# All matrix products with plain float32 operands in a low-pass convolution block

## The chip, the cores and the metric

The kernel runs on one core of a Trainium2 chip. The metric is the time of one execution on the device in microseconds (us). Before the change the median of three runs is 2578.18 us (2577.39 to 2587.52).

## The reference, cut to what matters

```python
xs = jnp.einsum('bhwc,dc->bhwd', x, W1) + b1      # x (16, 64, 64, 768) f32, W1 (192, 768)
xs = jax.nn.gelu(xs, approximate=False)
xs = fft_low(xs)    # |inverse 2-D FFT of the masked, shifted 2-D FFT| over h and w, per image and channel
xs = jnp.einsum('bhwd,cd->bhwc', xs, W2) + b2     # W2 (768, 192)
return x + xs
```

All tensors are float32. The mask keeps the 32 x 32 lowest frequencies, so the low-pass filter is a 64 x 64 matrix along w, another along h, and a rank-few correction (called corner in the code).

## The kernel before, in words

An image has 4096 positions of 768 channels. It is worked in 16 *pairs* of 128-position tiles (`PAIRS`), so there are 256 pairs over 16 images. A product with TensorE (PE) takes a stationary operand of up to 128 x 128 (loaded by a weight load, row PEld) and a moving operand of so many columns.

*Stage 1* (per pair, in three *units* of four 128-channel chunks, `UPP` = 3, `BLOCKS` = 4). `transpose_unit` (L254) transposes four 128 x 128 pieces of x with PE (L267) into one PSUM bank. ScalarE (ACT) copies the bank to `xt_hi` in the type fp32r (L373, `xt_hi_unit`), VectorE (DVE) computes the rest `xt_lo` (L461). `mm1_unit` (L270) then takes, for every chunk, one product of `xt_hi` with 384 columns (W1 high and W1 low side by side, L280) and one of `xt_lo` with 192 columns (W1 high, L281). Six chunks make one tile of the 192 hidden channels; there are twelve chunks in a pair. DVE adds the halves and b1 (L470, L475), ACT applies Gelu twice (L379, L380) to get `hid_hi` and the full value, DVE makes `hid_lo` (L480).

*Filter along w* (`filter_w_pair`, L284): three products of 384 columns (L290 to L292). ACT copies the result out (L385), SyncE (SP) writes it to DRAM (L201), and when all 16 pairs of an image are there it is read back with h and w swapped (`read_cols`, L208) in eight chunks. *Filter along h* (`filter_h_pair`, L304): three products of 128 columns with operands in **plain float32** (L314 twice, L316 once), the only ones beside the small corner sums (L298, L300) that are plain before the change. DVE adds the correction (L495).

*Stage 2*: ACT takes absolute values into `oa_hi`, `ob`, `ob1`, `y_abs` (L393 to L398), DVE makes the low parts (L502, L504, `split_lo_pair`), and `out_half` (L318) takes five products of 384 columns for each of the four output halves of a pair (L326, L327, L328, L331, L334). The bias b2 is a row of `w2b_lo`. DVE adds x (L513), SP stores (L221).

*Order.* Each engine runs a list written out by hand (`turn`): for step s of a turn and j = 0, 1, 2. `stage(i, s, lag)` gives the image and the pair that a stage works on at this step: stage 1 has lag 0, Gelu and filter w lag 1, reading back lag 17, filter h lag 18, low parts lag 19, output lag 20, store lag 21. In a full step PE runs in this order: at j = 0 a transpose unit (two units ahead), a first-product unit, one output half, filter h; at j = 1 a transpose unit, a first-product unit, filter w, one output half; at j = 2 a transpose unit, a first-product unit, two output halves. So PE works on two images at once. `turns` writes out the turns of images 0, 1 and 15 and the drain (turns 16 and 17); images 2 to 14 run in a hardware loop of 13 rounds. In turn 16 PE has only filter h and output. SP is one queue for all transfers: in a step it loads x for stage 1, stores, reads x for the addition (`load_xc`), issues the next read-back chunk at every second step, and writes filtered rows; a wait of any of them holds the ones behind.

Setup: W1, W2, b2 and the filter land in slots of `xc`, ACT and DVE split them into high and low parts there (L362, L364, L429 to L453), and the first loads of `xc` wait for that (`s_setup`).

Of the kernel before, what the change touches and what calls it, by code (L numbers as in the profile page):

```python
# [10 lines left out]
P = 128  # L11
# [21 lines left out]
SPLIT_LO = FILTER_H + 1  # L33
OUT = FILTER_H + 2
# [4 lines left out]
def lowpass_kernel(nc, x, w1t, b1, w2t, b2, identity, filter_w, filter_h, corner_table, out):  # L39
# [9 lines left out]
    with ctx:  # L49
# [10 lines left out]
        w1s = sb("w1s", [P, KC, 2 * D], F32R)  # L60
        w2a_hi = sb("w2a_hi", [P, C], F32R)
        w2a_lo = sb("w2a_lo", [P, C], F32R)
        w2b_hi = sb("w2b_hi", [P, C], F32R)
        w2b_lo = sb("w2b_lo", [P, C], F32R)
        ident = sb("ident", [P, P])
        b1_rows = sb("b1_rows", [P, D])
        fw_hi = sb("fw_hi", [P, P], F32R)
        fw_lo = sb("fw_lo", [P, P], F32R)
        fh = sb("fh", [P, P])
        corner_pat = sb("corner_pat", [P, 16])  # L70
        xt_hi = sb("xt_hi", [P, XT_SLOTS, BLOCKS * P], F32R)
        xt_lo = sb("xt_lo", [P, XT_SLOTS, BLOCKS * P], F32R)
        hid = sb("hid", [P, 2, 2, D])
        hid_hi = sb("hid_hi", [P, 2, 2, D], F32R)
        hid_lo = sb("hid_lo", [P, 2, 2, D], F32R)
# [5 lines left out]
        y_abs = sb("y_abs", [P, 2, 3, P])  # L81
        oa_hi = sb("oa_hi", [P, O_SLOTS, 2, P], F32R)
        oa_lo = sb("oa_lo", [P, O_SLOTS, 2, P], F32R)
        ob = sb("ob", [P, O_SLOTS, 2, P], F32R)
        ob1 = sb("ob1", [P, O_SLOTS, 2, P], F32R)


        w1f = xc[:, 7, :, :].rearrange("p t (k d) -> p (t k) d", d=D)[:, 0:KC, :]
        w2af, w2bf, b2f, fwf = xc[:, 0, 0, :], xc[:, 0, 1, :], xc[:, 1, 0, :], xc[:, 1, 1, 0:P]
# [13 lines left out]
        s_w1s = sem("w1_ready")  # L103
        s_w2_hi = sem("w2_hi_ready")
        s_setup = sem("setup_done")
        s_chain = sem("setup_chain")
# [7 lines left out]
        s_xhi = sem("xt_hi_ready")  # L114
        s_xlo = sem("xt_lo_ready")
        s_m1 = sem("mm1_unit_done")
        s_sum = sem("hid_summed")
        s_pre = sem("hid_pre_ready")
        s_gelu = sem("gelu_done")
        s_hlo = sem("hid_lo_ready")  # L120
# [9 lines left out]
        s_hi = sem("y_abs_and_hi_ready")  # L130
        s_alo = sem("oa_lo_ready")
        s_blo = sem("ob_lo_ready")
# [36 lines left out]
        def _(sp):  # L169
# [3 lines left out]
            def load_constants():  # L173
                const(fwf, filter_w)
                const(fh[:], filter_h)
                const(corner_pat[:], corner_table)
                const(w2af, w2t[0:P, :])
                for r in range(2):
                    const(w2bf[r * DB:(r + 1) * DB], w2t[P:D, :])
                for r in (64, 96):  # L180
                    const(b2f[r:r + 1], b2.rearrange("(a c) -> a c", a=1))
# [69 lines left out]
        def _(pe):  # L251
            pe.wait_ge(s_ident, 16)

            def transpose_unit(m, n):  # L254
# [8 lines left out]
                until(pe, s_xlo, UNITS, m, n - 1)  # L263
# [6 lines left out]
            def mm1_unit(m, n):  # L270
                if whole(m) and m == 0 and n == 0:
                    pe.wait_ge(s_w1s, 1)
                until(pe, s_xlo, UNITS, m, n + 1)
                for b in range(BLOCKS):
                    t, k = divmod(BLOCKS * n + b, KC)
                    if k == 0:
                        until(pe, s_pre, 2 * PAIRS, m, t - 1)
                    hi = xt_hi[:, n % XT_SLOTS, b * P:(b + 1) * P]
                    lo = xt_lo[:, n % XT_SLOTS, b * P:(b + 1) * P]
                    nc.tensor.matmul(ps_h[t % 2][:, 0:2 * D], hi, w1s[:, k, :], start=k == 0, stop=False)  # L280
                    ins = nc.tensor.matmul(ps_h[t % 2][:, D:2 * D], lo, w1s[:, k, 0:D], start=False, stop=k == KC - 1)  # L281
                ins.then_inc(s_m1, 1)

            def filter_w_pair(m, q):  # L284
                if whole(m) and m == 0 and q == 0:
                    pe.wait_ge(s_setup, 1)
                until(pe, s_hlo, PAIRS, m, q + 1)
                until(pe, s_fs, PAIRS, m, q)
                hi, lo = (t[:, q % 2, :, :].rearrange("p t d -> p (t d)") for t in (hid_hi, hid_lo))
# [28 lines left out]
            def out_half(m, r, u):  # L318
# [4 lines left out]
                a_hi, a_lo, b, b1h = (t[:, r % O_SLOTS, v, :] for t in (oa_hi, oa_lo, ob, ob1))  # L323
# [5 lines left out]
                if u == 0:  # L329
                    until(pe, s_alo, PAIRS, m, r + 1)  # L330
                nc.tensor.matmul(o, a_lo, w2a_hi[:, n], start=False, stop=False)  # L331
                if u == 0:
                    until(pe, s_blo, PAIRS, m, r + 1)
                nc.tensor.matmul(o, b, w2b_hi[:, n], start=False, stop=True).then_inc(s_o, 1)  # L334
# [23 lines left out]
        def _(act):  # L358
            def set_up_hi(q):
                act.wait_ge(s_const, 16 * 8)  # L360
                if q == 1:
                    nc.scalar.activation(w2a_hi[:], w2af, ACT.Copy).then_inc(s_w2_hi, 1)  # L362
                else:
                    nc.scalar.activation(w2b_hi[:], w2bf, ACT.Copy).then_inc(s_w2_hi, 1)  # L364

            def xt_hi_unit(m, n):
# [6 lines left out]
                nc.scalar.activation(xt_hi[:, n % XT_SLOTS, :], ps_xt[n % 2][:], ACT.Copy).then_inc(s_xhi, 1)  # L373

            def gelu_pair(m, q):
                until(act, s_pre, 2 * PAIRS, m, 2 * q + 2)
                until(act, s_f, PAIRS, m, q - 1)
                pre = hid[:, q % 2, :, :]
                nc.scalar.activation(hid_hi[:, q % 2, :, :], pre, ACT.Gelu)  # L379
# [7 lines left out]
            def split_hi_pair(m, r):  # L387
# [3 lines left out]
                until(act, s_blo, PAIRS, m, r - 1)  # L391
                yr, hi, hi1 = y[:, r % 2, :, :], ob[:, r % O_SLOTS, :, :], ob1[:, r % O_SLOTS, :, :]
                nc.scalar.activation(oa_hi[:, r % O_SLOTS, :, :], yr[:, 0:2, :], ACT.Abs)  # L393
                nc.scalar.activation(hi[0:DB, 0, :], yr[0:DB, 2, :], ACT.Abs)
                nc.scalar.activation(hi[DB:P, 1, :], yr[DB:P, 2, :], ACT.Abs)
                nc.scalar.activation(hi1[0:DB, 0, :], yr[0:DB, 2, :], ACT.Abs)
                nc.scalar.activation(hi1[0:DB, 1, :], yr[DB:P, 2, :], ACT.Abs)
                nc.scalar.activation(y_abs[:, r % 2, :, :], yr, ACT.Abs).then_inc(s_hi, 1)  # L398

            def turn(i, count):  # L400
                for s in range(count):
                    for j in range(UPP):
                        if whole(i) and i == 0 and s == 0 and j == 0:
                            for n in range(AHEAD):
                                xt_hi_unit(0, n)
                        if at := stage(i, s, 0):
                            xt_hi_unit(at[0], UPP * at[1] + j + AHEAD)
# [4 lines left out]
                        if j == 2 and (at := stage(i, s, FILTER_H)):  # L412
                            split_hi_pair(*at)
                        if whole(i) and i == 0 and s in (1, 2) and j == 2:
                            set_up_hi(s)
# [4 lines left out]
        def _(dve):  # L420
            chain = [0]

            def link(ins):
                chain[0] += 1
                ins.then_inc(s_chain, 1)
                dve.wait_ge(s_chain, chain[0])

            dve.wait_ge(s_w1, 16)
            link(nc.vector.tensor_copy(w1s[:, :, 0:D], w1f))  # L429
            nc.vector.tensor_tensor(w1s[:, :, D:2 * D], w1f, w1s[:, :, 0:D].bitcast(F32), ALU.subtract).then_inc(s_w1s, 1)  # L430

            def set_up_filters():
                dve.wait_ge(s_const, 16 * 8)
                link(nc.vector.tensor_copy(fw_hi[:], fwf))
                nc.vector.tensor_tensor(fw_lo[:], fwf, fw_hi[:].bitcast(F32), ALU.subtract).then_inc(s_setup, 1)

            def set_up_w2():
                nc.vector.memset(ob1[DB:P, :, :, :].bitcast(F32), 1.0)
                link(nc.vector.memset(w2b_lo[DB:P, :].bitcast(F32), 0.0))

            def set_up_w2a_lo():
                dve.wait_ge(s_w2_hi, 2)
                nc.vector.tensor_tensor(w2a_lo[:], w2af, w2a_hi[:].bitcast(F32), ALU.subtract)

            def set_up_w2b_lo():
                nc.vector.tensor_tensor(w2b_lo[0:DB, :], w2bf[0:DB], w2b_hi[0:DB, :].bitcast(F32), ALU.subtract)

            def set_up_b2_hi():
# [188 lines left out]
```

## Time and profile before

| | |
|---|---|
| runs | 2577.39, 2578.18, 2587.52 us |
| profiled execution, its own time | 2587.09 us |
| its span in the trace | 2585.3 us |
| mean granted TensorE clock | 0.985 |
| busy share of the span | PE 96%, PEld 95%, DVE 77%, ACT 49%, POOL (GpSimd) 14% |
| DMA | 710.34 MB, mean 275 GB/s |

The span is the time from the first to the last recorded instruction. A row of a group says line, engine, operation, output<-inputs, shapes, count, then busy us in all and mean ns of one, then idle time of the engine before them. PE products are pipelined: the duration of one is longer than the distance between the starts of two, and their ends are modelled, so what a product costs in a stream is read from starts, or from the chain, where a piece lasts until the next begins. A plain float32 product in the code stands in the trace as two records (L316: 256 products, 512 records); an fp32r product as one (L280: 3072 products, 3072 records).

### The profile page before, as it was taken

To read this page: it belongs to the slowest core of one execution; us is meant where nothing else is said; L and a number is where in the kernel's file an instruction comes from. 1 tells how busy PE (TensorE), PEld (TensorE's weight loads), DVE (VectorE), ACT (ScalarE), POOL (GpSimd) and SP (SyncE) were. 2 spreads that over 40 slices of the span, in tenths; PEclk is the share of its full clock that TensorE was granted. 3 is DMA by queue.
4 is the path that set the end of the run, shared out by engine and by line. 5 is a ranking of instruction groups with operands and counts; after the bars stand their busy time and mean duration, and the time that the engine had idled before them with its cause. 6 is when DMAs were issued, how large, how long until landed. Compare 5 with 4: busy or idle time off the path is not lost.

```text
span 2585.3 us, 55397 instructions
## 1 busy us (share of the span) xinstructions
PE 2479.2 (96%) x16736; PEld 2444.6 (95%) x16736; DVE 2000.3 (77%) x4123; ACT 1271.2 (49%) x3076; POOL 349.4 (14%) x628
## 2 busy tenths in 40 slices
PE   8999999999999999999999999999999999999977
PEld 7899999999999999999999999999999999999976
DVE  6688887878878787787878878788787887888855
ACT  4555554555545455454544545455454554555532
POOL 1211111111111111111111111111111111111100
PEclk9999999999999999999999999999999999999988
DMA  6688887888878788787887878778787887888775
GB/s 198 221 281 289 286 292 258 299 279 283 298 259 292 258 294 286 260 282 270 291 287 258 298 255 291 268 275 294 264 287 266 290 294 258 296 292 285 254 271 228
DMA packets 233562, 710.34 MB, mean 275 GB/s; under 512 B 18706, under 2 KB 85522, under 8 KB 233236
## 3 DMA queue, kind: packets, MB, share of 16 engines
q1 hardware_dynamic: 233236, 706.40, 77.9%
q8 instruction: 154, 2.52, 0.4%
q14 instruction: 172, 1.41, 0.2%
HBM read 454.67 MB, written 251.66 MB: 273 GB/s over the span
## 4 chain that ended last, share of the span: by engine, by line
PE 88%; DMA 4%; issue 4%; ACT 1%; DVE 1%; SPq 0%; POOL 0%; DVEq 0%; ACTq 0%; POOLq 0%
PE ps L280 21%; PE ps L267 12%; PE ps L281 10%; PE ps L326 7%; PE ps L328 7%; PE ps L327 6%; PE ps L331 6%; PE ps L334 6%; PE ps L314 4%; DMA cols<-filtered_rows 4%; PE ps L290 2%; PE ps L316 2%; PE ps L291 2%; PE ps L292 2%; DVE hid_lo L480 0%
## 5 line engine op out<-in xcount | busy, mean ns | idle before, releaser
L373 ACT ACTIVATE xt_hi<-ps 128x512 fp32r<-128x512 f32 x768 | 459.2, 598 | 1205.2 <-PE ps L267 1170.9
L280 PE MATMUL ps<-w1s,xt_hi 128*128 128x384 f32 x3072 | 987.6, 377 | 0.0
L461 DVE TENSOR_TENSOR xt_lo<-ps,xt_hi 128x512 fp32r<-128x512 f32 x768 | 529.9, 690 | 360.1 <-ACT xt_hi L373 346.7
L281 PE MATMUL ps<-w1s,xt_lo 128*128 128x192 f32 x3072 | 773.6, 252 | 0.0
L513 DVE TENSOR_TENSOR xc<-ps,xc 128x384 f32<-128x384 f32 x1024 | 569.4, 556 | 140.9 <-PE ps L334 118.7
L281 PEld LDWEIGHTS ps<-w1s,xt_lo 128*128 128x128 f32 x3072 | 591.1, 192 | 0.0
L280 PEld LDWEIGHTS ps<-w1s,xt_hi 128*128 128x128 f32 x3072 | 582.6, 190 | 0.0
L267 PE MATMUL ps<-ident,xa 128*128 128x128 f32 x3072 | 467.1, 275 | 25.0 <-issue 16.4
L267 PEld LDWEIGHTS ps<-ident,xa 128*128 128x128 f32 x3072 | 378.6, 142 | 46.1 <-issue 26.3
L326 PE MATMUL ps<-w2a_hi,oa_hi 128*128 128x384 f32 x1024 | 365.5, 357 | 0.4 <-DVE xc L513 0.4
L328 PE MATMUL ps<-w2b_lo,ob 128*128 128x384 f32 x1024 | 352.0, 344 | 0.0
L331 PE MATMUL ps<-w2a_hi,oa_lo 128*128 128x384 f32 x1024 | 351.1, 343 | 0.0
L327 PE MATMUL ps<-w2a_lo,oa_hi 128*128 128x384 f32 x1024 | 350.9, 343 | 0.0
L334 PE MATMUL ps<-w2b_hi,ob 128*128 128x384 f32 x1024 | 349.6, 341 | 0.0
L555 POOL TENSOR_TENSOR diff<-hid 128x192 f32<-128x192 f32 x240 | 151.4, 631 | 1103.4 <-ACT hid L380 1103.2
L504 DVE TENSOR_TENSOR ob<-y_abs,ob 64x128 fp32r<-64x128 f32 x512 | 252.8, 494 | 11.4
L559 POOL TENSOR_TENSOR corner_acc<-corner_acc,diff 128x192 f32<-128x192 f32 x240 | 142.9, 595 | 736.7 <-DMA cols<-filtered_rows 726.1
L326 PEld LDWEIGHTS ps<-w2a_hi,oa_hi 128*128 128x128 f32 x1024 | 195.7, 191 | 4.0 <-DVE xc L513 0.8
L327 PEld LDWEIGHTS ps<-w2a_lo,oa_hi 128*128 128x128 f32 x1024 | 197.0, 192 | 0.0
L475 DVE TENSOR_TENSOR hid<-ps,hid 128x192 f32<-128x192 f32 x512 | 183.1, 358 | 17.6
L334 PEld LDWEIGHTS ps<-w2b_hi,ob 128*128 128x128 f32 x1024 | 195.6, 191 | 0.0
L328 PEld LDWEIGHTS ps<-w2b_lo,ob 128*128 128x128 f32 x1024 | 195.4, 191 | 0.0
(50 smaller groups left out, 2714.5 us busy)
## 6 DMA issues: line engine op xcount, KB each, us to landing
xa<-x_dram SPq DMA_DIRECT2D x256, 768.0 KB, 4.8
xc<-x_dram SPq DMA_DIRECT2D x256, 768.0 KB, 7.0
out_dram<-xc SPq DMA_DIRECT2D x256, 768.0 KB, 5.1
filtered_rows<-filt SPq DMA_DIRECT2D x256, 192.0 KB, 2.1
cols<-filtered_rows SPq DMA_DIRECT2D x128, 384.0 KB, 7.4
xc<-w1t_dram SPq DMA_DIRECT2D x1, 576.0 KB, 6.0
xc<-w2t_dram SPq DMA_DIRECT2D x1, 384.0 KB
xc<-w2t_dram SPq DMA_DIRECT2D x2, 192.0 KB
```

The source lines that it names most:

```text
L267: ins = nc.tensor.transpose(ps_xt[n % 2][:, b * P:(b + 1) * P], src, ident[:])
L280: nc.tensor.matmul(ps_h[t % 2][:, 0:2 * D], hi, w1s[:, k, :], start=k == 0, stop=False)
L281: ins = nc.tensor.matmul(ps_h[t % 2][:, D:2 * D], lo, w1s[:, k, 0:D], start=False, stop=k == KC - 1)
L326: nc.tensor.matmul(o, a_hi, w2a_hi[:, n], start=True, stop=False)
L327: nc.tensor.matmul(o, a_hi, w2a_lo[:, n], start=False, stop=False)
L328: nc.tensor.matmul(o, b1h, w2b_lo[:, n], start=False, stop=False)
L331: nc.tensor.matmul(o, a_lo, w2a_hi[:, n], start=False, stop=False)
L334: nc.tensor.matmul(o, b, w2b_hi[:, n], start=False, stop=True).then_inc(s_o, 1)
L373: nc.scalar.activation(xt_hi[:, n % XT_SLOTS, :], ps_xt[n % 2][:], ACT.Copy).then_inc(s_xhi, 1)
L461: nc.vector.tensor_tensor(xt_lo[:, n % XT_SLOTS, :], ps_xt[n % 2][:], xt_hi[:, n % XT_SLOTS, :].bitcast(F32), ALU.subtract).then_inc(s_xlo, 1)
L504: ins = nc.vector.tensor_tensor(o[other, v, :], yr[own, 2, :], o[own, v, :].bitcast(F32), ALU.subtract)
L513: nc.vector.tensor_tensor(x_half, ps_o[u % 2][:, 0:HALF], x_half, ALU.add).then_inc(s_add, 1)
```

## The change

Every high and low part is gone. The operands are plain float32 tensors, the transposes stay. First product: per chunk one product of 192 columns instead of one of 384 and one of 192. Filter w: one product instead of three. Output half: two products of 384 columns instead of five; the second has 65 rows, row 64 being the bias b2 against a row of ones that DVE writes once. ACT runs one Gelu instead of two and three Abs instead of six; DVE runs one addition for the hidden value instead of two, and none of L461, L480, L502, L504. The output runs one step earlier (lag 19, store lag 20). The constants are loaded straight into their places, nothing is split in setup, and the first `xc` loads wait for nothing. Two waits are added: PE waits once for the ones (`s_ones`) and once for the constants; `hid_pre` now also waits for the filter product two pairs back (`s_f`).

```diff
-SPLIT_LO = FILTER_H + 1
-OUT = FILTER_H + 2
+OUT = FILTER_H + 1
 STORE = OUT + 1
...
-        w1s = sb("w1s", [P, KC, 2 * D], F32R)
-        w2a_hi = sb("w2a_hi", [P, C], F32R)
...
+        w1 = sb("w1", [P, KC, D])
+        w2a = sb("w2a", [P, C])
+        w2b = sb("w2b", [P, C])
...
             def load_constants():
-                const(fwf, filter_w)
+                const(fw[:], filter_w)
...
+                const(w2a[:], w2t[0:P, :])
+                const(w2b[0:DB], w2t[P:D, :])
+                const(w2b[DB:DB + 1], b2.rearrange("(a c) -> a c", a=1))
...
-                if whole(m) and m == 0 and r < XC_SLOTS:
-                    sp.wait_ge(s_setup, 2)
...
             def mm1_unit(m, n):
                 if whole(m) and m == 0 and n == 0:
-                    pe.wait_ge(s_w1s, 1)
-                until(pe, s_xlo, UNITS, m, n + 1)
+                    pe.wait_ge(s_w1, 16)
+                until(pe, s_xt, UNITS, m, n + 1)
...
-                    nc.tensor.matmul(ps_h[t % 2][:, 0:2 * D], hi, w1s[:, k, :], start=k == 0, stop=False)
-                    ins = nc.tensor.matmul(ps_h[t % 2][:, D:2 * D], lo, w1s[:, k, 0:D], start=False, stop=k == KC - 1)
+                    ins = nc.tensor.matmul(ps_h[t % 2][:, 0:D], xt[:, n % XT_SLOTS, b * P:(b + 1) * P], w1[:, k, :],
+                                           start=k == 0, stop=k == KC - 1)
...
-                nc.tensor.matmul(ps_f[:, 0:2 * D], fw_hi[:], hi, start=True, stop=False)
-                nc.tensor.matmul(ps_f[:, 0:2 * D], fw_lo[:], hi, start=False, stop=False)
-                nc.tensor.matmul(ps_f[:, 0:2 * D], fw_hi[:], lo, start=False, stop=True).then_inc(s_f, 1)
+                nc.tensor.matmul(ps_f[:, 0:2 * D], fw[:], hid[:, q % 2, :, :].rearrange("p t d -> p (t d)"),
+                                 start=True, stop=True).then_inc(s_f, 1)
...
                 if u == 0:
-                    until(pe, s_hi, PAIRS, m, r + 1)
-                nc.tensor.matmul(o, a_hi, w2a_hi[:, n], start=True, stop=False)
-                nc.tensor.matmul(o, a_hi, w2a_lo[:, n], start=False, stop=False)
-                nc.tensor.matmul(o, b1h, w2b_lo[:, n], start=False, stop=False)
...
-                nc.tensor.matmul(o, a_lo, w2a_hi[:, n], start=False, stop=False)
...
-                nc.tensor.matmul(o, b, w2b_hi[:, n], start=False, stop=True).then_inc(s_o, 1)
+                    until(pe, s_abs, PAIRS, m, r + 1)
+                nc.tensor.matmul(o, oa[:, r % O_SLOTS, v, :], w2a[:, n], start=True, stop=False)
+                nc.tensor.matmul(o, ob[0:DB + 1, r % O_SLOTS, v, :], w2b[0:DB + 1, n], start=False, stop=True).then_inc(s_o, 1)
...
-            def split_hi_pair(m, r):
+            def abs_pair(m, r):
...
+                nc.scalar.activation(oa[:, r % O_SLOTS, :, :], yr[:, 0:2, :], ACT.Abs)
+                nc.scalar.activation(ob[0:DB, r % O_SLOTS, 0, :], yr[0:DB, 2, :], ACT.Abs)
+                nc.scalar.activation(ob[0:DB, r % O_SLOTS, 1, :], yr[DB:P, 2, :], ACT.Abs).then_inc(s_abs, 1)
...
+            nc.vector.memset(ob[DB:DB + 1, :, :, :], 1.0).then_inc(s_ones, 1)
+
+            def hid_pre(m, t):
                 until(dve, s_m1, UNITS, m, -(-KC * (t + 1) // BLOCKS))
...
                     until(dve, s_acc, PAIRS, m, t // 2 - 1)
+                    until(dve, s_f, PAIRS, m, t // 2 - 1)
+                nc.vector.tensor_tensor(hid[:, t // 2 % 2, t % 2, :], ps_h[t % 2][:, 0:D], b1_rows[:], ALU.add).then_inc(s_pre, 1)
```

## Rows read from the trace of the kernel before

**Rows 1.** The page: span, and busy time, share, instructions of each engine.

```profile
span 2585.3 us, 55397 instructions
...
PE 2479.2 (96%) x16736; PEld 2444.6 (95%) x16736; DVE 2000.3 (77%) x4123; ACT 1271.2 (49%) x3076; POOL 349.4 (14%) x628
```

**Rows 2.** The page: the chain that ended last, share of the span by engine.

```profile
PE 88%; DMA 4%; issue 4%; ACT 1%; DVE 1%; SPq 0%; POOL 0%; DVEq 0%; ACTq 0%; POOLq 0%
```

**Rows 3.** Groups by line and shape on PE: busy us, mean ns | idle before.

```profile
L280 PE MATMUL ps<-w1s,xt_hi 128*128 128x384 f32 x3072 | 987.6, 377 | 0.0
L281 PE MATMUL ps<-w1s,xt_lo 128*128 128x192 f32 x3072 | 773.6, 252 | 0.0
L267 PE MATMUL ps<-ident,xa 128*128 128x128 f32 x3072 | 467.1, 275 | 25.0 <-issue 16.4 <-DMA xa<-x_dram 6.0 <-DVE xt_lo L461 2.5
...
L334 PE MATMUL ps<-w2b_hi,ob 128*128 128x384 f32 x1024 | 349.6, 341 | 0.0
L314 PE MATMUL ps<-fh,cols 128*128 128x128 f32 x1024 | 158.4, 277 | 32.4 <-DMA cols<-filtered_rows 25.9 <-issue 4.6 <-POOL cols_b L569 1.8
L316 PE MATMUL ps<-fh,cols_b 128*128 128x128 f32 x512 | 100.8, 279 | 0.0
```

**Rows 4.** The chain in order of time, one pair in mid-kernel: start us, us, what.

```profile
1000.87 0.43 PE ps L267 x4
1001.30 0.18 PE ps L280
1001.49 0.09 PE ps L281
...
1002.43 0.20 PE ps L326
1002.63 0.18 PE ps L327
...
1003.33 0.44 PE ps L314 x4
1003.77 0.22 PE ps L316 x2
...
1010.34 0.44 PE ps L267 x4
```

**Rows 5.** Timeline, a plain float32 product of 16 columns: start, us, engine, shapes.

```profile
109.75 0.30 PEld L298 LDWEIGHTS ps<-corner_pat,corner_acc 128*128 128x128 f32 x2
109.84 0.31 PE L298 MATMUL ps<-corner_pat,corner_acc 128*128 128x16 f32 x2
```

**Rows 6.** Two stretches: length, busy us (count) by engine, granted clock, DMA share, GB/s.

```profile
1000.00:1010.00 10.00, 10.00 (x70) 9.93 (x69) 8.19 (x17) 5.46 (x15) 0.61 (x1) 1.00 0.89 309
1039.60:1042.80 3.20, 3.20 (x11) 3.11 (x12) 2.26 (x6) 0.00 (x0) 0.00 (x0) 0.50 0.00 0
```

**Rows 7.** The chain in order of time, inside the second of these stretches.

```profile
1040.88 0.32 PE ps L326
```

**Rows 8.** Timeline where the loop goes round: [idle before <- what ended it].

```profile
1028.92 0.52 ACT L398 ACTIVATE y_abs<-y 128x384 f32<-128x384 f32 x1
...
1028.93 0.34 PE L334 MATMUL ps<-w2b_hi,ob 128*128 128x384 f32 x1
...
1030.63 0.65 PE L267 MATMUL ps<-ident,xa 128*128 128x128 f32 x4 [1.36 <-issue]
...
1035.86 0.60 ACT L373 ACTIVATE xt_hi<-ps 128x512 fp32r<-128x512 f32 x1 [6.42 <-PE ps L281]
...
1039.56 0.68 PE L290 MATMUL ps<-hid_hi,fw_hi 128*128 128x384 f32 x1 [4.03 <-DVE hid_lo L480]
```

**Rows 9.** Timeline in the drain: a read-back issued, and the product that needs it.

```profile
2488.17 0.91 SPq L214 DMA_DIRECT2D cols<-filtered_rows  x1
...
2495.75 1.11 PE L314 MATMUL ps<-fh,cols 128*128 128x128 f32 x4 [3.97 <-DMA cols<-filtered_rows]
```

**Rows 10.** The page, DMA queues: packets, MB, share of 16 engines.

```profile
q1 hardware_dynamic: 233236, 706.40, 77.9%
```

**Rows 11.** Timeline at the start: the first product of stage 1.

```profile
11.24 0.67 PE L280 MATMUL ps<-w1s,xt_hi 128*128 128x384 f32 x1
```

More of the change, by code:

```diff
@@ L80, in lowpass_kernel @@
         y = sb("y", [P, 2, 3, P])
[L81 to L89, printed above, removed]
+        oa = sb("oa", [P, O_SLOTS, 2, P])
+        ob = sb("ob", [P, O_SLOTS, 2, P])
         ps = [ctx.enter_context(nc.psum_tensor(f"ps{n}", [P, 512], F32)) for n in range(8)]
@@ L358, in _, with xt_unit @@
         def _(act):
[L359 to L366, printed above, removed]
+            def xt_unit(m, n):
                 if n >= UNITS:
@@ L372, in xt_hi_unit @@
                 until(act, s_m1, UNITS, m, n - XT_SLOTS + 1)
-                nc.scalar.activation(xt_hi[:, n % XT_SLOTS, :], ps_xt[n % 2][:], ACT.Copy).then_inc(s_xhi, 1)
+                nc.scalar.activation(xt[:, n % XT_SLOTS, :], ps_xt[n % 2][:], ACT.Copy).then_inc(s_xt, 1)
             def gelu_pair(m, q):
                 until(act, s_pre, 2 * PAIRS, m, 2 * q + 2)
-                until(act, s_f, PAIRS, m, q - 1)
                 pre = hid[:, q % 2, :, :]
-                nc.scalar.activation(hid_hi[:, q % 2, :, :], pre, ACT.Gelu)
                 nc.scalar.activation(pre, pre, ACT.Gelu).then_inc(s_gelu, 1)
@@ L385, in stage_filtered @@
                 nc.scalar.activation(filt[:, q % 2, :, :].rearrange("p t d -> p (t d)"), ps_f[:, 0:2 * D], ACT.Copy).then_inc(s_fs, 1)
-            def split_hi_pair(m, r):
+            def abs_pair(m, r):
                 until(act, s_o, 4 * PAIRS, m, 4 * (r - O_SLOTS + 1))
                 until(act, s_y, PAIRS, m, r + 1)
[L391 to L398, printed above, removed]
+                yr = y[:, r % 2, :, :]
+                nc.scalar.activation(oa[:, r % O_SLOTS, :, :], yr[:, 0:2, :], ACT.Abs)
+                nc.scalar.activation(ob[0:DB, r % O_SLOTS, 0, :], yr[0:DB, 2, :], ACT.Abs)
+                nc.scalar.activation(ob[0:DB, r % O_SLOTS, 1, :], yr[DB:P, 2, :], ACT.Abs).then_inc(s_abs, 1)
             def turn(i, count):
@@ L412, in turn @@
                         if j == 2 and (at := stage(i, s, FILTER_H)):
-                            split_hi_pair(*at)
-                        if whole(i) and i == 0 and s in (1, 2) and j == 2:
-                            set_up_hi(s)
+                            abs_pair(*at)
             turns(act, turn)
@@ L420, in _ @@
         def _(dve):
[L421 to L448, printed above, removed]
-                nc.vector.tensor_copy(w2b_lo[DB:DB + 1, :], b2f[DB:DB + 1])
-            def set_up_b2_lo():
-                link(nc.vector.tensor_copy(w2b_lo[96:97, :], b2f[96:97]))
-                nc.vector.tensor_tensor(w2b_lo[96:97, :], b2f[96:97], w2b_lo[96:97, :].bitcast(F32), ALU.subtract).then_inc(s_setup, 1)
-            def xt_lo_unit(m, n):
-                if n >= UNITS:
-                    m, n = m + 1, n - UNITS
-                    if whole(m) and m >= IMAGES:
-                        return
-                until(dve, s_xhi, UNITS, m, n + 1)
-                nc.vector.tensor_tensor(xt_lo[:, n % XT_SLOTS, :], ps_xt[n % 2][:], xt_hi[:, n % XT_SLOTS, :].bitcast(F32),
-                                        ALU.subtract).then_inc(s_xlo, 1)
-            def hid_sum(m, t):
+            nc.vector.memset(ob[DB:DB + 1, :, :, :], 1.0).then_inc(s_ones, 1)
+            def hid_pre(m, t):
                 until(dve, s_m1, UNITS, m, -(-KC * (t + 1) // BLOCKS))
@@ L497, in y_pair @@
                                         ALU.add if r % 2 == 0 else ALU.subtract).then_inc(s_y, 1)
-            def split_lo_pair(m, r):
-                until(dve, s_hi, PAIRS, m, r + 1)
-                yr, hi, o = y_abs[:, r % 2, :, :], oa_hi[:, r % O_SLOTS, :, :], ob[:, r % O_SLOTS, :, :]
-                nc.vector.tensor_tensor(oa_lo[:, r % O_SLOTS, :, :], yr[:, 0:2, :], hi.bitcast(F32), ALU.subtract).then_inc(s_alo, 1)
-                for v, (own, other) in enumerate(((slice(0, DB), slice(DB, P)), (slice(DB, P), slice(0, DB)))):
-                    ins = nc.vector.tensor_tensor(o[other, v, :], yr[own, 2, :], o[own, v, :].bitcast(F32), ALU.subtract)
-                ins.then_inc(s_blo, 1)
             def add_half(m, r, u):
```

78 lines of the change are left out of this document (14 added, 64 removed).

## Prediction

> **What bounds the kernel now.** I read the page first. PE is busy for 96% of the span and the next engine, DVE, for 77% [rows 1]; busy PE time alone proves little, since the records of pipelined products overlap, so the chain of waits came second: 88% of it lies on PE, the rest is waiting for DMA and for issue, and DVE and ACT have 1% each [rows 2]. Then the groups on PE by shape [rows 3], and for what a product costs in a stream the chain in order of time over one pair [rows 4]. There PE never waits: a pair lasts from 1000.87 to 1010.34, which is 9.47 us, at full granted clock [rows 6]. 256 pairs x 9.47 = 2424 us. The profiled execution took 2587.1 us, so 163 us lie outside the steady work (start, loop ends, drain). The kernel is bound by PE's stream of columns, and the whole question is what a plain float32 product costs there.
>
> **The pair before, in pieces** [rows 4]. A transpose unit takes 0.43, the four chunks behind it run from 1001.30 to 1002.43, 1.13 us; a unit is 1.56 us and a pair has three, 4.68. An output half runs from 1002.43 to 1003.33, 0.90 us for five products, four halves 3.60. Filter h is 0.44 + 0.22 = 0.66. The rest, 9.47 - 4.68 - 3.60 - 0.66 = 0.53, is filter w with three products. So an fp32r product of 384 columns costs 0.176 to 0.18 us in a stream.
>
> **What a plain product costs.** The trace has them at 128 columns only. Each appears as two records, L314 at 0.44/4 and L316 at 0.22/2, that is 0.11 us a record or pass [rows 4]. Two readings give 0.11. One: the weight load sets it. With 16 columns the two loads lie 0.30 minus one load of 0.19, 0.11 us, apart, though the two passes start only 0.05 apart (0.31 minus 0.26 for one) [rows 5]; so a load costs 0.11 whatever the columns. Two: a pass gives every column two column times; 2 x 128 at 2.4 GHz is 0.107. What tells them apart is how long one record lasts. In fp32r 192 columns last 252 ns and 384 last 341 ns, 0.46 ns a column, so 128 would last 222 ns. The plain pass of 128 columns lasts 277 to 279 ns [rows 3], what fp32r would show at about 250 columns. (The transposes, also on float32, show 275.) That is a modelled end, but it speaks clearly for two column times a pass, four for the product.
>
> The Trainium skill, page "FP8 and Floating Point Precision", section "TensorE Precision Notes", says that true FP32 takes four passes through the array; by it alone a product of 192 columns would be 4 x 192 / 2.4 = 320 ns and one of 384 columns 640 ns, an estimate close to mine below, where fp32r takes a quarter of it. The trace shows two records a product, not four, and 128 columns cannot decide, because the load hides the rate there.
>
> Bounds of a pass. Below: the load, 0.11 us, or one column time at the fp32r price, 0.176 for 384 columns. Above: twice the fp32r price for the same columns, 0.352 for 384 and 0.177 for 192. The fp32r price carries a surcharge: 384 columns at 2.4 GHz are 0.160, and 0.176 is 10% more, while at the granted clock 0.50 (1.2 GHz) the same product takes 0.32, exactly its columns [rows 6, 7]. The plain pass at 128 columns shows at most 0.11 for 0.107, so hardly any surcharge. I take column time plus 0.005 us: 0.165 for 192 columns, 0.325 for 384. Each is longer than a load, so the loads stay hidden beneath.
>
> **The pair after.** Removed: all fp32r products. Stage 1: 12 chunks x 2 passes x 0.165 = 3.96, before 3 x 1.13 = 3.39: +0.57. Output: 4 halves x 2 products x 2 passes x 0.325 = 5.20, before 3.60: +1.60. The second product has 65 rows instead of 128; I give it no discount, since every pass of the trace is priced by columns. Filter w: 2 x 0.325 = 0.65, before 0.53: +0.12. Transposes 3 x 0.44 = 1.31 and filter h 0.66 stay. Sum 3.96 + 5.20 + 0.65 + 1.31 + 0.66 = 11.78 us a pair, x 256 = 3016 us.
>
> **The other engines.** ACT loses one Gelu and three Abs of its 1271 us, DVE five groups of its 2000 us (the low parts and one addition); both had room at 9.47 us a pair (5.0 and 7.8 us) [rows 1] and have more at 11.78. This saving is hidden and worth nothing in steady state. The transfers keep their bytes, 77.9% of 2585 us [rows 10], about 2014 us, over a longer time. The added wait of `hid_pre` for the filter product two pairs back stands for a product that PE finished a step before; behind it on DVE are `y_pair` and the additions, and it costs nothing unless DVE runs a step ahead, which its waits for `s_m1` exclude. The single waits for the ones and constants are over long before their first use. Output one step earlier: PE does the same amount per pair in the same place of the step, its input from ACT (three Abs, ready in j = 2) has two output halves and a unit of cover. The end comes one step earlier, but that step held no more than one pair's work in either case: counted at nothing, with 2 us either way. `xc` loads at the start no longer wait for setup: off PE's path.
>
> **What lies around the steady work** (163 us before).
> - *Loop ends.* Twelve times the loop goes round. There PE sits for 1.4 us, ACT comes back 6.4 us after its last Abs, and filter w then waits 4.0 us for ACT and the DVE backlog, after which PE ran for 3.2 us at half clock and lost 1.6 [rows 6, 8]. About 6.6 us each, 79 in all. After the change ACT ends its step about 2 us before PE (its work in j = 2 is 2.1 us after the transposes, PE's 3.9), so its return falls 2 us earlier, there are no low parts to catch up on, and PE has 0.44 + 1.32 + 1.30 + 0.66 + 0.44 + 1.32 = 5.5 us of work before filter w instead of 4.9. I expect only PE's own 1.5 us to stay: 18 us. If that cover fails, up to 79 again.
> - *Drain.* Read-backs are issued one step ahead. One issued at 2488.17 serves a product at 2495.75, 7.6 us later, and PE stood 4.0 us [rows 9]. An image has eight such reads; seven waits like this one are 28 us, with some clock lost behind each I take 37. A step of PE there grows from 4.3 to 5.9 us and the order of the queue is the same, so a wait of about 1.7 us is left per read, 8 x 1.7 = 14 us.
> - *Start*: the first product comes at 11.24 [rows 11]; it no longer waits for the split of W1, some 3 us less. With the filling of the stages and the first read-back 15 us, before 21. End 5 us. What I could not place is about 20 us; I keep it.
> Sum 18 + 14 + 15 + 5 + 20 = 72. The profiled execution comes to 3016 + 72 = 3088 us. The median of the runs before was 0.35% under the profiled one (2578.18 against 2587.09); that gives 3077, rounded to **3080 us**, 19% slower.
>
> **Rivals.**
> *A, one column time a pass.* If a plain pass streams at one column per cycle, and 0.11 at 128 columns is only the load, a unit is 0.44 + 8 x 0.11 = 1.32, a half 4 x 0.176 = 0.70, filter w 0.35, and the pair 3.96 + 2.82 + 0.35 + 0.66 = 7.8 us, 1995 us in all. Then read-backs come late in every second step (9 us of path against 7.8 of work, some 130 us), the loop ends cost their old 79 and the rest 30: 2230 us, faster. It decides from a pass of 384 columns below about 0.25 us. For it: 0.11 fits the load exactly. Against: 277 ns. Chance 0.07.
> The Trainium skill, page "TensorE: Matmul & The Clock Gate", section "Weight-path perf modes — Fast Weight Load (FWL) and DoubleRow", has the array process one element per cell per cycle regardless of element width; read as a rule for a pass it is rival A, with 0.160 us for 384 columns. The trace's 277 ns at 128 columns disagrees with it.
>
> *B, the surcharge comes along.* Twice the fp32r price: 24 x 0.177 + 16 x 0.352 + 0.70 + 1.31 + 0.66 = 12.55, x 256 = 3213, + 75 = 3290 us. For it: fp32r products of both widths carry 10%. Against: the plain pass of 128 columns would be 0.117, and it is 0.11. Chance 0.12.
>
> *C, the loop ends stay as they are*, because the half clock or ACT's return does not move: 3088 + 61 = 3150 us, with chance 0.15, inside the range.
>
> *D, the change does not bring what it says* (plain products merge into one record, or a wait takes over): within 0.5% or anywhere; 0.01.
>
> **How the numbers follow.** The forecast itself, 3030 to 3130, has 0.65; with C 0.80. Low end: passes at bare column time (pair 11.6 us, 2972) + 60 = 3030. High end: half of B's surcharge, 3115 + 85 = 3200. Outside are A and most of B. A measurement of this kernel tells about 0.5% from no change. Faster 0.07 (A), same 0.01, slower 0.92.
>
> **What would show it.** Records: L267 3072, first product 6144, output 4096 in two lines, filter w 512. In the chain over one pair: passes of the first product 0.165 apart, of the output 0.325, a pair of 11.8 us; record durations near 335 ns at 192 columns and 495 at 384. PE idle before filter w at loop ends under 1 us. DVE under 40% busy. I am wrong if the output's passes start 0.18 apart (A) or 0.35 (B), or if PE shows idle time inside the pairs.

## The result, and the profile after

The change makes the kernel slower: 3036.35 us (3034.08 to 3038.87) against 2579.89 us, a ratio of 1.175, 95% interval 1.1727 to 1.1775. Forecast were 3080 us, 19% slower, and a range from 3030 to 3200. The profiled execution took 3034.77 us. The figures of the kernel before are here the median of four runs, one more than stood before the prediction.

Page of the kernel after, as [rows 1, 2 and 10]:

```profile
span 3033.0 us, 48049 instructions
...
PE 3012.4 (99%) x15456; PEld 2365.8 (78%) x15456; DVE 878.4 (29%) x1809; ACT 897.1 (30%) x2050; POOL 335.8 (11%) x628
...
q1 hardware_dynamic: 233154, 706.20, 67.1%
q8 instruction: 152, 2.49, 0.3%
q14 instruction: 19, 0.16, 0.0%
...
PE 98%; DMA 2%; issue 0%; SPq 0%; DVE 0%; ACT 0%; ACTq 0%
```

DVE fell from 2000 to 878 us and ACT from 1271 to 897, and none of it bought time: 98% of the chain is PE. The groups on PE, as [rows 3]:

```profile
L252 PE MATMUL ps<-w,xt 128*128 128x192 f32 x6144 | 1127.2, 327 | 0.0
L297 PE MATMUL ps<-w2a,oa 128*128 128x384 f32 x2048 | 829.7, 487 | 0.0
L298 PE MATMUL ps<-w2b,ob 65*128 65x384 f32 x2048 | 829.2, 485 | 0.0
L241 PE MATMUL ps<-ident,xa 128*128 128x128 f32 x3072 | 463.5, 273 | 6.7 <-DMA xa<-x_dram 6.0 <-issue 0.7
L261 PE MATMUL ps<-hid,fw 128*128 128x384 f32 x512 | 207.0, 486 | 0.0
```

The counts are those foreseen: two records a product. A record of 192 columns lasts 327 ns where fp32r had 252, one of 384 columns 487 where it had 341. What a pass costs in the stream is in the chain over one pair, as [rows 4]:

```profile
1001.12 0.44 PE ps L241 x4
1001.57 1.30 PE ps L252 x8
1002.87 0.65 PE ps L297 x2
1003.51 0.65 PE ps L298 x2
...
1008.49 0.45 PE ps L284 x4
1008.93 0.22 PE ps L286 x2
...
1010.89 0.65 PE ps L261 x2
...
1012.83 0.22 PE ps L241 x2
```

Eight passes of 192 columns take 1.30 us, 0.1625 each; two of 384 take 0.645, 0.3225 each. At the granted clock of 2.4 GHz that is two column times (0.160 and 0.320) plus 2.5 ns, in both widths. Rows do not matter: L298 with 65 of them costs what L297 with 128 does. The pair lasts from 1001.12 to 1012.83, 11.71 us; 256 of them are 2998 us, so 37 us lie outside where the kernel before had 163.

A loop end after, as [rows 8] (timeline):

```profile
1026.57 0.31 ACT L349 ACTIVATE ob<-y 64x128 f32<-64x128 f32 x1
...
1028.06 0.81 PE L298 MATMUL ps<-w2b,ob 65*128 65x384 f32 x2
1028.90 0.65 PE L241 MATMUL ps<-ident,xa 128*128 128x128 f32 x4
...
1029.66 0.60 ACT L330 ACTIVATE xt<-ps 128x512 f32<-128x512 f32 x1 [2.78 <-PE ps L241]
...
1034.39 0.81 PE L261 MATMUL ps<-hid,fw 128*128 128x384 f32 x2
```

ACT ends (1026.88) 1.2 us before PE's last product of the round starts (1028.06), and on the other side it waits for PE's transposes, not PE for it. PE loses 0.2 us here (1028.06 + 0.65 would be 1028.71), and filter w starts without a wait. The mean granted clock of the execution is 1.00.

### The profile page after: what moved, and what is told of

It reads as the page before. It is cut to its first block, busy times and chain, and to the rows that moved or that the text cites. A ratio compares the mean times of both kernels' runs of the same rounds, so it can differ in the third digit from the quotient of the medians.

```text
span 3033.0 us, 48049 instructions
## 1 busy us (share of the span) xinstructions
PE 3012.4 (99%) x15456; PEld 2365.8 (78%) x15456; DVE 878.4 (29%) x1809; ACT 897.1 (30%) x2050; POOL 335.8 (11%) x628
## 4 chain that ended last, share of the span: by engine, by line
PE 98%; DMA 2%; issue 0%; SPq 0%; DVE 0%; ACT 0%; ACTq 0%
PE ps L252 33%; PE ps L297 21%; PE ps L298 21%; PE ps L241 11%; PE ps L261 5%; PE ps L284 4%; PE ps L286 2%; DMA cols<-filtered_rows 1%; DMA xa<-x_dram 0%; PE ps L270 0%; DMA filtered_rows<-filt 0%; PE ps L268 0%; DVE xc L404 0%; ACT filt L340 0%; SPq L149 0%
## 5 line engine op out<-in xcount | busy, mean ns | idle before, releaser
L252 PE MATMUL ps<-w,xt 128*128 128x192 f32 x6144 | 1127.2, 327 | 0.0
L330 ACT ACTIVATE xt<-ps 128x512 f32<-128x512 f32 x768 | 458.5, 597 | 2011.4 <-PE ps L241 2011.4
L252 PEld LDWEIGHTS ps<-w,xt 128*128 128x128 f32 x6144 | 981.7, 190 | 0.3
L297 PE MATMUL ps<-w2a,oa 128*128 128x384 f32 x2048 | 829.7, 487 | 0.0
L298 PE MATMUL ps<-w2b,ob 65*128 65x384 f32 x2048 | 829.2, 485 | 0.0
L298 PEld LDWEIGHTS ps<-w2b,ob 65*128 65x128 f32 x2048 | 390.3, 191 | 272.4
L297 PEld LDWEIGHTS ps<-w2a,oa 128*128 128x128 f32 x2048 | 373.5, 190 | 142.3
L380 DVE TENSOR_TENSOR hid<-ps,b_rows 128x192 f32<-128x192 f32 x512 | 183.2, 358 | 854.2 <-PE ps L252 854.2
L261 PE MATMUL ps<-hid,fw 128*128 128x384 f32 x512 | 207.0, 486 | 0.0
L284 PE MATMUL ps<-fh,cols 128*128 128x128 f32 x1024 | 156.1, 274 | 9.5 <-DMA cols<-filtered_rows 6.8
```

The source lines that it names most:

```text
L252: ins = nc.tensor.matmul(ps_h[t % 2][:, 0:D], xt[:, n % XT_SLOTS, b * P:(b + 1) * P], w1[:, k, :], start=k == 0, stop=k == KC - 1)
L261: nc.tensor.matmul(ps_f[:, 0:2 * D], fw[:], hid[:, q % 2, :, :].rearrange("p t d -> p (t d)"), start=True, stop=True).then_inc(s_f, 1)
L284: nc.tensor.matmul(ps_y[:, v * P:(v + 1) * P], col[:, v, 0:P], fh[:], start=v == 0, stop=False)
L297: nc.tensor.matmul(o, oa[:, r % O_SLOTS, v, :], w2a[:, n], start=True, stop=False)
L298: nc.tensor.matmul(o, ob[0:DB + 1, r % O_SLOTS, v, :], w2b[0:DB + 1, n], start=False, stop=True).then_inc(s_o, 1)
L330: nc.scalar.activation(xt[:, n % XT_SLOTS, :], ps_xt[n % 2][:], ACT.Copy).then_inc(s_xt, 1)
```

## Experiments

Each ran beside the kernel before, whose median lay between 2585 and 2592 us then (2580 beside the kernel after); ratios and differences are to the one that ran beside. Two runs of different groups can so be compared to some 0.4% only, 10 us. First the change taken apart, one of its three kinds of product at a time.

**w_plain**, filter w alone:

```diff
-                nc.tensor.matmul(ps_f[:, 0:2 * D], fw_hi[:], hi, start=True, stop=False)
-                nc.tensor.matmul(ps_f[:, 0:2 * D], fw_lo[:], hi, start=False, stop=False)
-                nc.tensor.matmul(ps_f[:, 0:2 * D], fw_hi[:], lo, start=False, stop=True).then_inc(s_f, 1)
+                nc.tensor.matmul(ps_f[:, 0:2 * D], fw[:], hid[:, q % 2, :, :].rearrange("p t d -> p (t d)"),
+                                 start=True, stop=True).then_inc(s_f, 1)
```

> The kernel before with only the filter along w in plain float32 (one product of 384 columns instead of three; one Gelu, no hid_lo). Pass theory (two column times a pass plus about 2.5 ns): PE's pair grows by 0.645 - 0.53 = 0.115 us, 29 us over 256 pairs. Loop theory (the loop ends cost the kernel before about 79 us because ACT fetches its loop code again; they go where its code gets short enough to be kept): with 16 activations and 16 waits fewer in a round either the instruction queue's packets fall from 172 to about 20 and the time is 2580 + 29 - 79 = 2530, or they stay and only the Gelu and hid_lo leave the wait, 12 x 1.1 = 13 us: 2596. Rival (slack theory: the fetch never mattered, only the work behind it): 2596 whatever the packets show.

Measured 2595.33 us, ratio 1.0043 (1.0027 to 1.006), 10.7 us more than the 2584.64 beside it, where 16 more were expected. ACT's instruction queue q14 still shows 158 packets: the hope of 2530 failed. With the packets there, both theories say 2596, so the time does not part them. The trace does. PE's wait before filter w is gone, but another one has come, before filter h, and ACT is no longer late at a loop end:

```profile
PE ps L308 <- issue: 35.9, 14, 3.6
```

```profile
716.20 0.60 ACT L367 ACTIVATE xt_hi<-ps 128x512 fp32r<-128x512 f32 x1 [1.51 <-PE ps L263]
```

"issue" means that the profile shows nothing that PE waited for. Twelve of the fourteen waits lie at the loop ends.

**m1_plain**, the first product alone:

```diff
-                    nc.tensor.matmul(ps_h[t % 2][:, 0:2 * D], hi, w1s[:, k, :], start=k == 0, stop=False)
-                    ins = nc.tensor.matmul(ps_h[t % 2][:, D:2 * D], lo, w1s[:, k, 0:D], start=False, stop=k == KC - 1)
+                    ins = nc.tensor.matmul(ps_h[t % 2][:, 0:D], xt[:, n % XT_SLOTS, b * P:(b + 1) * P], w1[:, k, :],
+                                           start=k == 0, stop=k == KC - 1)
```

> The kernel before with only the first product in plain float32 (12 products of 192 columns a pair, no xt_lo, one addition). Pass theory: 12 x (0.325 - 0.2825) = 0.51 us a pair more, +131 us. ACT's list is unchanged, so its loop code is fetched again at every round and the loop ends keep the wait for ACT (they lose only DVE's xt_lo, 0.7 us each, and may have somewhat more PE work over them, 0.4 us): 2580 + 131 - 15 = 2696. Rival (all of the gain at the loop ends comes from DVE having less to catch up): 2580 + 131 - 60 = 2650.

Measured 2664.93 us, ratio 1.0313 (1.029 to 1.0336), 80 us more, between the two. The pair is 9.94 us, 0.47 more, which is 120 us, so 40 came back outside the pairs. ACT's list is the same (157 packets in q14), and ACT is late as before, here at one loop end:

```profile
579.89 0.60 ACT L366 ACTIVATE xt<-ps 128x512 f32<-128x512 f32 x1 [6.59 <-PE ps L262]
```

What went is DVE's xt_lo and its backlog, and PE has more work; PE's wait for hid_lo fell from 43.6 to 18.9 us.

**out_plain**, the output alone:

```diff
-OUT = FILTER_H + 2
+OUT = FILTER_H + 1
...
+                nc.tensor.matmul(o, oa[:, r % O_SLOTS, v, :], w2a[:, n], start=True, stop=False)
+                nc.tensor.matmul(o, ob[0:DB + 1, r % O_SLOTS, v, :], w2b[0:DB + 1, n], start=False, stop=True).then_inc(s_o, 1)
```

> The kernel before with only the output products in plain float32 (two of 384 columns a half, three Abs, output one step earlier). Pass theory: 4 x (4 x 0.3225 - 0.90) = 1.56 us a pair more, +400 us. Loop theory: ACT loses 48 activations a round; if its packets fall to about 20, the loop ends cost only PE's 1.5 us: 2580 + 400 - 61 - drain 20 = 2899; if not, about 2940. Rival (a pass of the 65-row product is cheaper than of 128 rows): under 2800.

Measured 2919.03 us, ratio 1.1296 (1.1268 to 1.1323), 334 us more, for a pair of 11.11 us (+1.64, 420 us). 86 us came back. The rival of cheaper 65-row passes is out. The loop theory missed: the packets did not fall, and the time lies between its two numbers. The page, and PE's longest wait:

```profile
q14 instruction: 156, 1.28, 0.1%
```

```profile
PE ps L304 <- issue: 25.1, 14, 6.4
```

So about three quarters of the loss (334 of 456 us) is the output, where two plain products (1.29 us) take the place of five fp32r ones (0.90). The three parts alone add up to 425 us, 31 less than the whole change: their pairs add up to it (2.22 of 2.24 us), but each run alone brings back part of the same loss outside the pairs, 18 + 40 + 86 = 144 us where only 126 can be had.

The waits of PE before a product, kernel before and after (waited for: us in all, times, longest):

```profile
PE ps L290 <- DVE hid_lo L480: 43.6, 18, 4.2
PE ps L314 <- DMA cols<-filtered_rows: 25.9, 8, 4.9
PE ps L267 <- issue: 16.4, 12, 1.8
```

```profile
PE ps L284 <- DMA cols<-filtered_rows: 6.8, 6, 1.8
PE ps L241 <- DMA xa<-x_dram: 6.0, 1, 6.0
PE ps L284 <- issue: 2.6, 2, 2.3
PE ps L241 <- issue: 0.7, 3, 0.4
```

Why are the first and third gone? After shows 19 packets in ACT's instruction queue q14, before 172: ACT's loop code seems no longer to be fetched at each round. **act_pad** gives ACT three useless Abs a pair, so its list is long again:

```diff
+                nc.scalar.activation(scrap[0:DB, 0, 0, :], yr[0:DB, 2, :], ACT.Abs)
+                nc.scalar.activation(scrap[0:DB, 0, 1, :], yr[0:DB, 2, :], ACT.Abs)
+                nc.scalar.activation(scrap[:, 1, :, :], yr, ACT.Abs).then_inc(s_abs, 1)
```

> The kernel after with three more Abs a pair on ACT into a scrap tile, as many activations as the kernel before has there; nothing reads them, ACT stays under half busy. Loop theory: ACT's code is again too long to be kept, the packets of its instruction queue come back (from 19 towards 170), and ACT returns some 6 us after its last activation of a round. With 5.6 us of PE work before filter w, and ACT now done at most 1 us before PE, filter w waits 0 to 2 us at each of 12 loop ends: 3036 to 3065. Slack theory (fetch costs nothing, nor does it come back): 3036, packets 19.

Measured 3040.79 us, ratio 1.177 (1.1744 to 1.1796). That is 4 us over after, less than two groups of runs can tell apart (after has 1.1751, 1.1727 to 1.1775). Its page and a loop end:

```profile
q14 instruction: 81, 0.66, 0.1%
```

```profile
1028.88 0.51 ACT L353 ACTIVATE scrap<-y 128x384 f32<-128x384 f32 x1
1031.68 0.60 ACT L331 ACTIVATE xt<-ps 128x512 f32<-128x512 f32 x1 [2.29 <-PE ps L242]
```

Packets come back in part, but ACT starts 2.3 us after its last operation's end, not 6.4, released by PE's transposes, and PE never waits for it. This does not settle the loop theory, for the list is not as long as before: one Gelu is still missing, so ACT has 176 activations a round and not 192. The traces of all six kernels say more. At the twelve loop ends ACT's first copy starts this long after the end of PE's transposes:

| kernel | activations a round | q14 packets | ACT's copy behind the transposes, us | loop ends in all, us |
|---|---|---|---|---|
| before | 192 | 172 | 1.5 to 4.8 | 79 |
| m1_plain | 192 | 157 | 0.3 to 5.4 | 53 |
| w_plain | 176 | 158 | 0.1 | 66 |
| act_pad | 176 | 81 | 0.1 | 5 |
| out_plain | 144 | 156 | 0.1 | 28 |
| after | 128 | 19 | 0.1 | 3 |

(The last column is by how much the three pairs around each loop end are longer than others, by the starts of the transposes, less the 6.5 us that the same pairs show with the loop written out.) Of these six ACT is late in the two with 192 activations a round and in none with fewer, and the count of packets does not say which. But ACT in time is not enough: in w_plain and out_plain PE itself then stands before filter h (1.8 to 3.6 and 0.9 to 2.0 us each time), and why it does there and not in after or act_pad no run shows.

**before_unrolled** and **after_unrolled** take the loop ends away:

```diff
-            with eng.Fori(2, IMAGES - 1) as i:
-                turn(i, PAIRS)
+            for i in range(2, IMAGES - 1):
+                turn(i, PAIRS)
```

> The kernel before with images 2 to 14 written out instead of a loop of 13 rounds; nothing else. Loop-end theory: the twelve loop ends cost 6.6 us each, which go: 2580 - 79 = 2501 us, PE idle before filter w gone. Rival (instruction fetch stalls straight code as well): 2560 to 2600.

> The kernel after, written out in the same way. Loop-end theory: its loop ends cost 0.1 to 0.7 us of PE each, so 3 to 6 us: 3031 us. Rival (the longer code costs it something): 3036 or more.

Measured 2503.24 us, ratio 0.9667 (0.964 to 0.9695), and 3032.82 us, ratio 1.1717 (1.1683 to 1.1751). The loop ends cost 85 us before, and after next to nothing: 4 us between the medians, again less than two groups can tell apart, and 3 us by the starts of the pairs. Waits of PE in before_unrolled:

```profile
PE ps L314 <- DMA cols<-filtered_rows: 26.0, 8, 5.4
...
PE ps L290 <- DVE hid_lo L480: 5.6, 6, 1.1
```

The wait for hid_lo fell from 43.6 to 5.6, the one for read-backs stayed. **before_early** takes that one:

```diff
+                    if (at := stage(i, s, READ_COLS)) and at[1] == 0:
+                        read_cols(at[0], 0)
-                    if (at := stage(i, s, READ_COLS)) and at[1] % 2 == 0:
+                    if (at := stage(i, s, READ_COLS - 2)) and at[1] % 2 == 0 and at[1] > 0:
                         read_cols(at[0], at[1] // 2)
```

> The kernel before with the read-back chunks 1 to 7 issued two steps earlier in SP's queue (chunk 0 stays, it must wait for the last rows). Drain theory: PE's seven waits of 3 to 5 us in the drain (28 us, and up to 10 of lost clock) go, the loop ends stay: 2582 - 36 = 2546 us. Rival (the DMA rate or DVE, 4.2 us a pair there, bounds the drain): under 15 us gained.

Measured 2548.73 us, ratio 0.9838 (0.9789 to 0.9887), 38 us less (29 to 55). The waits of PE there:

```profile
PE ps L292 <- DVE hid_lo L482: 46.4, 18, 4.4
PE ps L316 <- DMA cols<-filtered_rows: 2.7, 1, 2.7
```

One of eight waits for a read-back is left, and the loop ends are as they were. Both edits together, **best**:

> before_unrolled and before_early together, high and low parts kept: the two losses lie in different places, so they add: 2503 - 36 = 2467 us, with PE at 98% or more of the span and 256 x 9.47 = 2424 us of it in products. Rival (the DMA share, 0.80 in before_unrolled, begins to hold x and read-backs back): 2490 or more.

Measured 2471.21 us, ratio 0.9557 (0.9519 to 0.9594). The two gains nearly add (85 + 38 = 123 expected, 116 measured), PE is busy for 99% of the span, and 2424 of the 2471 us are 256 pairs at 9.47. This beats both kernels with the arithmetic of before.

**m1_64** asks where the weight load takes over:

```diff
-                    ins = nc.tensor.matmul(ps_h[t % 2][:, 0:D], xt[:, n % XT_SLOTS, b * P:(b + 1) * P], w1[:, k, :],
+                    ins = nc.tensor.matmul(ps_h[t % 2][:, 0:DB], xt[:, n % XT_SLOTS, b * P:(b + 1) * P], w1[:, k, 0:DB],
```

> The kernel after with 64 instead of 192 columns in each product of the first stage (128 of the 192 hidden channels are left out and filled by repetition). Tells where the weight load takes over from the columns. Load theory: a pass of 64 columns would be 64/1.2 = 53 ns, but the load of its 128 columns takes 108 ns, so passes start 0.108 apart; 24 x (0.1625 - 0.108) = 1.31 us a pair less, 335 us: 2701 us. Rival (plain passes follow their columns alone, loads run two ahead): 0.056 apart, 24 x 0.1065 = 2.56 us a pair less: 2381 us.

Measured 2735.86 us, ratio 1.0577 (1.0544 to 1.0609). The chain has two units of it:

```profile
1003.31 0.44 PE ps L241 x4
1003.75 0.84 PE ps L252 x8
...
1006.61 0.44 PE ps L241 x4
...
1013.80 0.44 PE ps L241 x4
```

A pair is 10.49 us, 1.22 less than 11.71, over 24 passes 0.051 each: from 0.1625 down to 0.112, twice what 64 columns need. That is the distance of two loads of 128 columns, as [rows 5] have it. Where the loads have 64 columns, in the corner sums, four passes of 8 columns take 0.22 us, 0.055 each (chain of out_plain):

```profile
1009.89 0.22 PE ps L290 x4
```

So the floor goes with the load and is no fixed cost of a pass. The 0.11 us at 128 columns before the change could not tell a rate, and the record's duration did. (The time fell by 300 us where 335 were expected: the pair gives 312, with 0.112 for 0.108, and 50 us lie outside the pairs instead of 37.)

**hi_only** replaces each plain product of after by one fp32r product (shown against the kernel before, the output products only):

```diff
-                nc.tensor.matmul(o, a_hi, w2a_lo[:, n], start=False, stop=False)
-                nc.tensor.matmul(o, b1h, w2b_lo[:, n], start=False, stop=False)
...
-                nc.tensor.matmul(o, b, w2b_hi[:, n], start=False, stop=True).then_inc(s_o, 1)
+                nc.tensor.matmul(o, b, w2b_hi[0:DB, n], start=False, stop=True).then_inc(s_o, 1)
```

> The kernel before with the high parts alone: one fp32r product wherever the kernel after has one plain product (192 columns in the first stage, two of 384 a half with 64 rows in the second, one in filter w), output one step earlier; all low parts and the bias b2 are left out. The same list of products as after, so it prices plain against fp32r one for one, and it is what rival A of the prediction would have given. fp32r theory: 192 columns are bound by the load, 0.109 (not 0.088), 384 columns 0.176: pair 3 x 0.88 + 4 x 0.35 + 0.18 + 0.66 = 4.9 us, PE 1250 us. Then the transfers bind: 710 MB at the rate at which 16 engines would be full (309 GB/s at 0.89 busy, so about 345) are 2060 us: 2060 to 2250. Rival (DMA share does not bind, read-backs do): 9 us for every two pairs and above, 1300 to 1600 us.

Measured 2474 to 2535 us in four runs; both expectations missed. PE's granted clock was 0.72 on average in the profile, so only the order and the count of its records can be set beside other runs, not their durations. The weight loads of the two output products (groups: busy, mean ns | idle before):

```profile
L310 PEld LDWEIGHTS ps<-w2a_hi,oa_hi 128*128 128x128 f32 x1024 | 254.5, 249 | 75.1 <-issue 74.4 <-DVE xc L439 0.2 <-ACT ob L371 0.2
L311 PEld LDWEIGHTS ps<-w2b_hi,ob 64*128 64x128 f32 x1024 | 231.5, 226 | 275.3 <-issue 275.3
```

Before the load of a 64-row operand PEld is idle each of the 1024 times, 0.27 us on average, until about the end of the product before it. The load behind it is held as well (timeline, where the granted clock was 0.50):

```profile
1547.17 0.29 PEld L311 LDWEIGHTS ps<-w2b_hi,ob 64*128 64x128 f32 x1 [0.44 <-issue]
1547.79 0.29 PEld L255 LDWEIGHTS ps<-ident,xa 128*128 128x128 f32 x2 [0.33 <-issue]
```

**hi_65** gives it one row more, the bias row that after has:

```diff
-                nc.tensor.matmul(o, b, w2b_hi[0:DB, n], start=False, stop=True).then_inc(s_o, 1)
+                nc.tensor.matmul(o, b, w2b_hi[0:DB + 1, n], start=False, stop=True).then_inc(s_o, 1)
```

> The run hi_only with 65 rows instead of 64 in the second output product (row 64 is the bias, as in after); low parts are left out. In hi_only the load of the 64-row product began only when the product before it had ended (0.33 us of PEld idle before each of the 1024), so a half took about 0.65 us at full clock instead of 0.35. Row theory: the load of a 64-row operand isn't taken ahead, one of 65 rows is: PEld idle before that line goes from 275 us to under 20, products 0.176 apart. The time falls by 1024 x 0.2 to 0.3 us of PE only where PE is on the path; read-backs hold the rest: 2300 to 2450 us. Rival (the gap comes from waiting for the additions of DVE): PEld idle and 2518 us stay.

Measured 2348.61 us, ratio 0.9094 (0.9051 to 0.9138), and in the same group:

```profile
L309 PEld LDWEIGHTS ps<-w2b_hi,ob 65*128 65x128 f32 x1024 | 217.1, 212 | 0.0
```

Only 64 and 65 rows were tried, so it is shown that one row more is enough, not why.

**hi_best** adds the two edits of best:

> hi_65 (high parts alone, low parts left out) with the read-back chunks 1 to 7 issued two steps earlier and the loop written out. In hi_65 45% of the chain is read-back and PE waits 0.7 ms before filter h. Transfer theory: with the read-backs early the bound passes to the 16 DMA engines: 0.822 x 2346 = 1930 us of work, seldom fuller than 0.9 on average: 2060 to 2150 us. Rival (PE stays below full clock and each step keeps a wait): 2250 or more.

Measured 1815.20 us, ratio 0.6999 (0.6975 to 0.7023), below every expectation. Its page:

```profile
span 1813.0 us, 30022 instructions
...
PE 1418.1 (78%) x10080; PEld 1348.3 (74%) x10080; DVE 835.1 (46%) x1812; ACT 992.9 (55%) x2308; POOL 338.5 (19%) x628
...
q1 hardware_dynamic: 233154, 706.20, 98.9%
```

Now the transfers are the bound: they are busy for 98.9% and hold 65% of the chain, PE 26%. (Loop and read-backs were changed together here, so the gain of each is not known.) The same bytes had 77.9% of 2585 us before, 2014 us, and here 1793: a share of busy DMA time is no fixed amount of work. This kernel drops the low parts, so it computes with less precision than either of the two; it is a comparison, not a replacement.

## Why the prediction was right

*The bound.* Right: PE before and after, and the other engines' savings in steady state bought nothing [rows 1, 2].

*The price of a plain pass.* Two column times, right, and the step that carried the sign. The durations of [rows 3] decided it: records of 128, 192 and 384 columns now last 274, 327 and 487 ns (335 and 495 foreseen), 0.83 ns a column, two column times, where fp32r shows 0.46. m1_64 confirms the other half of the argument, that 0.11 us is the load. The four passes that the Trainium skill states for true FP32 (page "FP8 and Floating Point Precision", section "TensorE Precision Notes") agree with the time, as two records of two column times each. I took 5 ns over the column time; it is 2.5. A pair came to 11.71 instead of 11.78, 18 us in all. Rival A (0.25 us or less) and rival B (0.35) are both excluded by 0.3225. (Had A been true, hi_65, which runs the same list of products at the fp32r price, puts the time at 2349 us and not at A's 2230: faster still, but PE waits 703 us before filter h there, and I gave late read-backs 130.) That plain passes lack fp32r's 10% surcharge (0.176 for 0.160) is shown; where the surcharge comes from was not tried.

*The parts.* Foreseen a pair: first product +0.57, output +1.60, filter w +0.12. Measured alone: +0.47, +1.64, +0.11. The first is 0.10 high: 24 passes carried 2.5 ns too many (0.06), and the product behind each of the three units took 0.20 us before [rows 4] and takes 0.17 to 0.18 in m1_plain.

*Loop ends.* 79 us before, right: before_unrolled gives 85. For after I kept 18; it is 3 to 4, and rival C is out. The step that failed is "I expect only PE's own 1.5 us to stay". PE loses 0.1 to 0.5 us at most of them; why its own restart got shorter I can't say, its instruction queue has as many packets (152 for 154). I had ACT return as late as before, only from an earlier end, and covered by more PE work. It isn't late at all after the change, nor in w_plain, act_pad and out_plain, so the cover was not what did it. More work and less backlog do count where ACT is late: m1_plain leaves ACT alone, and 26 of 79 us at the loop ends come back. What makes an engine late there stays open: PE's own stops in w_plain and out_plain speak against ACT's list as the only cause.

*Drain.* 37 us before, right (before_early: 38). After, I kept 14; PE's starts there are late by 8.3 us in all over seven reads, and no clock is lost (granted 1.00 from 2921 to 3024 us). The longer output of a step does it, as foreseen: PE waits 25.8 us for read-backs in m1_plain, 6.6 in out_plain.

*The rest.* I carried 20 us that I could not place into the sum, and 37 outside the pairs were measured in all, 72 forecast. These 35 us and the 18 of the pairs are the whole miss of 53 (3088 against 3034.77). Scaling by 0.9965 to the median hid 11 of it; the profiled run after stood at its median, so nothing speaks for such a factor.

*How near the miss was.* The price of a pass, which decides between faster and slower, was read from the trace and not guessed. The size was less safe: the pair and what lies outside the pairs were both put too high, and 3036 us lies only 6 us above the low end of the range. That end rests on a slip, too: passes at bare column time give a pair of 11.57 us and 2962, not 2972, and with 60 more 3022. It held because the pair is dearer than that by 0.14 us, 36 us in all, and only 23 us of the 60 were not needed.

## What to carry to other kernels

Price a product by its passes times columns, with the weight load as a floor: five fp32r products of 384 columns (0.90 us) are cheaper than two plain float32 ones (1.29), and three of them (0.53) than one (0.65). Work taken from engines that are not the bound pays only where the bound waits for them: here at twelve loop ends. The waits of the drain shrank for another reason, because PE's own steps grew longer. Both losses can be had back without giving up precision, by writing the loop out and issuing read-backs earlier (2471 us).

## What the runs showed of the hardware that I had not expected

- The load of a 64-row stationary operand was not taken ahead of the running product (0.27 us idle each, 1024 times, at a mean granted clock of 0.72), one of 65 rows was (0.0). The added row costs nothing in the trace: both output products of hi_65 start 0.18 us apart at full clock, and here the row also carries the bias.
- Each of the two records of a plain product with 192 or 384 columns costs its columns at half rate plus 2.5 ns; fp32r costs 10% over its columns at full clock [rows 4] and nothing at half clock [rows 7].
- At a loop end ACT came back late with 192 activations a round (up to 4.8 us behind the transposes before the change, 5.4 in m1_plain), and not in the kernels with 176, 144 and 128. Its instruction transfers do not tell this: 157 packets in m1_plain, where it is late, 158 in w_plain, where it is not.
